# Projections as 32-column matmuls, and layer 1 with two exponentials a tile and two VectorE passes

## What is computed

```python
# layer 0: attention, softmax within blocks of 256 keys, 4 heads of 64
q, k, v = x @ Wq.T + bq, x @ Wk.T + bk, x @ Wv.T + bv
scores = clip(q k / sqrt(64), -10, 10);  scores = where(mask == 0, -10, scores)
ctx = softmax(scores over each 256 keys) @ v, summed over the 8 blocks
x1 = layernorm(x + layernorm(ctx @ Wo.T + bo + x) * gamma + beta)
# layer 1: graph attention
Wh = x1 @ W;  e = leaky_relu(s_i[:, None] + s_j[None, :], 0.2)
h = softmax(where(adj or diagonal, e, -inf)) @ Wh
out = layernorm(x1 + elu(h))
```

## Time and profile before

| | us |
|---|---|
| median of 3 runs | 4188.16 (4187.67 to 4192.0) |
| the profiled execution | 4188.57 |
| its span | 4186.4 |
| PE busy | 3834.5 (92%) |
| DVE busy | 3188.7 (76%) |
| ACT busy | 2463.5 (59%) |
| POOL busy | 2460.5 (59%) |
| mean granted TensorE clock | 0.970 of 2.4 GHz |

### The profile page before, as it was taken

How to read it: one execution, slowest core, us unless ns; L and a number is a source line. 1 busy time by engine, 2 the same in 40 slices (tenths; PEclk the granted TensorE clock), 3 DMA queues, 4 the chain that set the end, 5 groups by cost and what they waited for, 6 DMA issues and landing times. The chain is left out here.

```text
span 4186.4 us, 61904 instructions
## 1 busy us (share of the span) xinstructions
PE 3834.5 (92%) x20868; PEld 1843.7 (44%) x20868; DVE 3188.7 (76%) x3845; ACT 2463.5 (59%) x3554; POOL 2460.5 (59%) x1293
## 2 busy tenths in 40 slices
PE   6999999999999999999999999935888898888888
PEld 2333333333333333333333333225676676676766
DVE  6676776676677577677677667857998999989997
ACT  3565565556566566566566556624566566575666
POOL 2776776677677677677667667822434444344344
PEclk9999999999999999999999999967999999999999
DMA  5000000010001000000000000051011010110000
GB/s 205 1 31 11 21 31 11 11 42 11 11 12 41 11 12 31 21 11 31 11 21 32 11 11 21 11 208 39 26 45 52 21 46 25 41 51 21 31 31 31
DMA packets 106398, 140.44 MB, mean 34 GB/s; under 512 B 3793, under 2 KB 87633, under 8 KB 104017
## 3 DMA queue, kind: packets, MB, share of 16 engines
q1 hardware_dynamic: 104816, 135.80, 9.7%
q10 hardware_dynamic: 1248, 0.40, 0.1%
HBM read 102.63 MB, written 33.55 MB: 33 GB/s over the span
## 5 line engine op out<-in xcount | busy, mean ns | idle before, releaser
L368 ACT ACTIVATE probs<-probs 128x1024 f32<-128x1024 f32 x1024 | 1080.6, 1055 | 1006.0 <-DVE probs L614 975.4
L614 DVE SCALAR_TENSOR_TENSOR probs<-sc_ps,clip_hi 128x1024 f32<-128x1024 f32 x1024 | 1202.8, 1216 | 600.3 <-PE sc_ps L439 579.6
L267 POOL TENSOR_TENSOR psums<-probs 128x1024 f32<-128x1024 f32 x512 | 1244.6, 2452 | 164.1 <-ACT probs L368 164.1
L1102 PE MATMUL out_ps<-wh,e 128*128 128x257 f32 x4096 | 984.2, 394 | 208.4 <-ACT e L1029 201.5
L439 PE MATMUL sc_ps<-q_cols,k_cols 64*128 64x512 f32 x4096 | 1023.1, 618 | 24.4 <-DVE probs L614 12.4
L455 PE MATMUL ctx_ps<-probs,v_rows 128*32 128x512 f32 x8192 | 982.5, 597 | 1.2 <-DVE seg_ctx L537 1.2
L1102 PEld LDWEIGHTS out_ps<-wh,e 128*128 128x128 f32 x4096 | 789.7, 196 | 377.2 <-ACT e L1029 177.7
L278 POOL TENSOR_TENSOR ctx_t<-ctx_t,seg_ctx 128x1024 f32<-128x1024 f32 x224 | 532.1, 2376 | 671.4 <-DVE seg_ctx L537 671.3
L439 PEld LDWEIGHTS sc_ps<-q_cols,k_cols 64*128 64x128 f32 x4096 | 353.2, 186 | 697.1 <-issue 569.9
L903 POOL TENSOR_TENSOR e<-e,mask 128x512 f32<-128x512 f32 x160 | 247.6, 1547 | 549.2 <-DVE e L1224 549.2
L1029 ACT ACTIVATE e<-e 128x512 f32<-128x512 f32 x512 | 319.0, 623 | 404.9 <-DVE e L1240 292.8
(11 more groups left out here) (85 smaller groups left out, 2776.4 us busy)
## 6 DMA issues: line engine op xcount, KB each, us to landing
x_cols<-in_xT SPq DMA_DIRECT2D x8, 2048.0 KB, 10.1
probs<-in_adjT SPq DMA_DIRECT2D x16, 1024.0 KB, 8.3
x_rows<-in_x SPq DMA_DIRECT2D x32, 512.0 KB, 5.2
x<-res SPq DMA_DIRECT2D x32, 512.0 KB, 3.3
x_in<-x SPq DMA_DIRECT2D x8, 2048.0 KB, 11.0
x_res<-x SPq DMA_DIRECT2D x32, 512.0 KB, 4.4
out<-h SPq DMA_DIRECT2D x32, 512.0 KB, 3.2
e<-in_adjT SPq DMA_DIRECT2D x8, 1024.0 KB, 9.4
```

The costliest lines, as they stand in the source:

```text
L267: pool.tensor_tensor(psums[:, q % 2, pair, :], probs[:, (SJ * q) % RING, pair, :], probs[:, (SJ * q + 1) % RING, pair, :], ALU.add).then_i ...
L368: act.activation(probs[:, n % RING, pair, :], probs[:, n % RING, pair, :], ACT.Exp, scale=DH ** -0.5).then_inc(s_exp, 1)
L614: dve.scalar_tensor_tensor(out=probs[:, n % RING, pair, :], in0=sc_ps[:, p, :, :], scalar=-LIM, in1=clip_hi[:, j, c * CW:(c + 1) * CW][:, ...
L1102: last = pe.matmul(out_ps[:, bank(c, t), 0:F + 1], e[:, n % ERING, t * P:(t + 1) * P], wh[:, p, j, 1:F + 2], start=(j == 0), stop=(j == JB ...
```

## The change

**Layer 0, TensorE.** Every matmul of a projection with 128 columns of weights becomes four with 32, one for each quarter of the output partitions, with the same streamed operand. The result and what reads it stay as they were.

```diff
                     for k in range(KB):
-                        last = pe.matmul(prj_ps[:, :], wk[:, k, p * P:(p + 1) * P],
-                                         x_cols[:, k, c * CW:(c + 1) * CW], start=(k == 0), stop=(k == KB - 1))
+                        for g in range(P // QUAD):
+                            at = p * P + g * QUAD
+                            last = pe.matmul(prj_ps[quad(g), :], wk[:, k, at:at + QUAD],
+                                             x_cols[:, k, c * CW:(c + 1) * CW], start=(k == 0), stop=(k == KB - 1))
...
                     for z in range(HALVES):
-                        last = pe.matmul(prj_ps[:, 0:F], ctx_t[:, c % 2, z, t * P:(t + 1) * P], wo[:, z, :],
-                                         start=(z == 0), stop=(z == HALVES - 1))
+                        for g in range(P // QUAD):
+                            i = t * P + g * QUAD
+                            last = pe.matmul(prj_ps[quad(g), 0:F], ctx_t[:, c % 2, z, i:i + QUAD], wo[:, z, :],
+                                             start=(z == 0), stop=(z == HALVES - 1))
```

```diff
-                act.wait_ge(s_mm, count(b, STEPS, n + 1))
-                act.activation(e[:, n % ERING, :], low[:, p, c * CW:(c + 1) * CW], ACT.Identity,
-                               bias=s_fifth[:, p, j:j + 1]).then_inc(s_lin, 1)
+                act.wait_ge(s_max, count(b, STEPS, n + 1))
+                act.activation(e_low[:, n % LRING, :], low[:, p, c * CW:(c + 1) * CW], ACT.Exp,
+                               bias=s_fifth[:, p, j:j + 1]).then_inc(s_lo, 1)
+                act.wait_ge(s_mm, count(b, STEPS, n + 1))
+                act.activation(e[:, n % ERING, :], best[:, p, c * CW:(c + 1) * CW], ACT.Exp,
+                               bias=wh[:, p, j, 0:1]).then_inc(s_hi, 1)
...
-                        act.activation(e[:, n % ERING, :], e[:, n % ERING, :], ACT.Exp).then_inc(s_e, 1)
...
-                dve.wait_ge(s_lin, count(b, STEPS, n + 1))
-                dve.scalar_tensor_tensor(out=tile, in0=best[:, p, c * CW:(c + 1) * CW],
-                                         scalar=wh[:, p, j, 0:1], in1=tile, op0=ALU.add, op1=ALU.max)\
-                   .then_inc(s_max, 1)
+                dve.wait_ge(s_lo, count(b, STEPS, n + 1))
+                dve.wait_ge(s_hi, count(b, STEPS, n + 1))
+                dve.tensor_tensor(tile, tile, e_low[:, n % LRING, :], ALU.max).then_inc(s_max, 1)
...
-                        if j in ON_DVE:
-                            dve.wait_ge(s_max, count(b, STEPS, n + 1))
-                            dve.tensor_tensor(tile, tile, mask[:, j, c * CW:(c + 1) * CW], ALU.add)\
-                               .then_inc(s_log, 1)
+                        dve.wait_ge(s_max, count(b, STEPS, LRING + n + 1))
+                        dve.scalar_tensor_tensor(out=tile, in0=mask[:, j, c * CW:(c + 1) * CW], scalar=0.0,
+                                                 in1=tile, op0=ALU.max, op1=ALU.min).then_inc(s_e, 1)
```

```diff
+                dve.tensor_scalar(piece.bitcast(F32), piece, 0, 2 * BIG, ALU.is_gt, ALU.mult).then_inc(s_flag, 1)
+                dve.wait_ge(s_flag, i + 1)
                 dve.tensor_scalar(mask[:, 4 * q:4 * q + 4, c * CW:(c + 1) * CW],
-                                  stages[i % 4].rearrange("p (a i) -> p a i", a=4),
-                                  0, -BIG, ALU.is_le, ALU.mult).then_inc(s_mask, 1)
+                                  piece.bitcast(F32).rearrange("p (a i) -> p a i", a=4),
+                                  -BIG, None, ALU.add).then_inc(s_mask, 1)
...
+            def residual(b, c):
+                dve.wait_ge(s_elu, count(b, NC, c + 1))
+                dve.wait_ge(s_xr[c % 2], count(b, 16 * (NC // 2), 16 * (c // 2 + 1)))
+                dve.scalar_tensor_tensor(out=h[:, c % 2, :, :], in0=h[:, c % 2, :, :], scalar=-1.0,
+                                         in1=x_res[:, c % 2, :, :], op0=ALU.add, op1=ALU.add).then_inc(s_r, 1)
```

92 lines of the change are left out of this document (33 added, 59 removed).

## The result

The changed kernel takes **4034.72 us** in the median of 4 runs (4033.95 to 4037.52), beside 4189.58 (4187.67 to 4192.0) of the kernel before on the same chip: a ratio of 0.9631, interval 0.9615 to 0.9648, 155 us less. The forecast was 4018, with a range of 3985 to 4082.

What follows compares the result with a forecast made beforehand. TensorE was taken to bound layer 0, layer 1's D and the last batch, VectorE A to C. 4188.57 - 58 (layer 0) - 114 (VectorE) - 9 (TensorE) + 11 (mask) = 4018.6, given as 4018 us, range 3985 to 4082.

Steps and rivals of the forecast that it cites:

- Layer 0: Projections on TensorE: 32-column sets save the change of form, 0.195 us in 306 uses; -58 us, between 0 and -62.
- rival 4: Layer 0 projections: a set of four costs 0.43 us whatever it streams; 220 us longer, 4238, chance 0.05.
- Rival 3: Layer 0: 32-column sets lose against full instructions, 0.03 us in each of 1464 sets, 44 us: 4062; chance 0.04.
- Rival 2: Layer 0: time between forms belongs to any new group of 128-column weights and comes back elsewhere; no gain, 4076, chance 0.05.
- The mask: Before layer 1's first tile: one more VectorE pass for each of 16 pieces; +11 us, between 9 and 20.
- A: Layer 1, tiles 19 to 34, bound by VectorE: 19.8 + 4.7 + 9 x 2.26 = 44.8 instead of 51.1 us, plus 0.6 for ScalarE.
- D: Layer 1, tiles 3 to 18 with most preparations, bound by TensorE: stays at 34.9 us.
- B: Layer 1, tiles 35 to 50, bound by VectorE: 36.0 instead of 43.0 us, with 5 maxima, plus 0.6 for ScalarE.
- C: Layer 1, tiles 51 to 2, bound by VectorE: 34.7 instead of 39.5 us, 1 for the reduction included, plus 0.6 for ScalarE.
- last batch: Layer 1, nothing to prepare, bound by TensorE: from 30.3 to between 27.7 and 28.5 us a chunk; -9 us.
- Rival 1: Layer 1: VectorE waits for ScalarE, 3.6 instead of 0.6 us in 21 stretches; 63 us back, 4081, chance 0.12.
- Rival 5: Layer 1 without waits for ScalarE and the cap at 0.60 us: 14 and 13 us better, 3991; chance 0.12.

Runs made afterwards that it cites:

- 64-column kernel: The kernel before with each projection matmul cut into two of 64 columns; 4174.45 us, ratio 0.9963.
- mask_one_pass: The changed kernel with each mask piece made in one pass instead of two; 4025.33 us, ratio 0.9609.
- kernel with one moved maximum: The changed kernel with only the maximum of tile 18 moved in front of the reciprocals in the second chunk; 4027.37 us, ratio 0.9615.
- no_reduction: The changed kernel without GpSimd's reduction over partitions, each partition using its own maximum, for timing only; 4014.46 us, ratio 0.9577.

## Why the prediction was right or wrong

**Layer 0: right.** -58 forecast, -59.4 measured in the trace, -62 alone. k and q took 1.74 (forecast 1.75), v 1.75, o 0.89, the contexts behind 1.83. The price without a row, a set of 256 columns, was the lower of its bounds, and rival 4 (0.43 whatever streams) fell with it. Rival 3 fell too. The Trainium skill's 2.38 times for three column tiles (page "TensorE: Matmul & The Clock Gate", section "Measured speedup vs the span model") is not what this kernel shows: a set of four takes 0.43 us for 512 columns in f32, as one full instruction does, so the four lose nothing beside each other. Wrong in part was the cause. The prediction said that between two forms there is a time to pay, and that it was all of the 0.19. Of 0.197 us, 0.080 are the width of the first load, as the 64-column kernel shows. Rival 2's idea was thus right for a part of it, but not its consequence, as the narrow load stays narrow. The Trainium skill, page "TensorEngine Tiling (Array Packing)", section "Key Properties", says that changing the tiling mode drains TensorE. What is left, 0.093 us for leaving the full form and 0.097 for leaving the 64-column one, agrees with it; the page has no figure, and no run here tells a drain from another cause.

**The mask: right**, +11.2 for +11, and shown by `mask_one_pass`. Between the terms it was off by 1 us each way: the eight late pieces cost 10.1 (forecast 9) and the eight early ones 0.9 (forecast 1.6).

**A: the count was wrong.** The step "19.8 + 4.7 + 9 x 2.26" missed one: A has 10 `maximum` passes. The one of tile 18 stands behind the reciprocals in VectorE's order, on A's side of my cut. So D has one and not two. That is 2.26 more; tile passes at 1.20 a tile instead of 1.24 take 0.6 back, and the 0.6 us for ScalarE were not needed. Forecast 45.4 with that charge, measured 46.4: 7 us in 7 batches, and 1.6 more in the two A behind the loop's branch (47.8 and 49.3; before 53.1 and 51.8). The kernel with one moved maximum shows it: with 9, A takes 44.5.

**B: the reduction was put in the wrong stretch and at the wrong size.** The step "C: ... + 1 for the reduction that still runs beside it" should have been in B with 3.4 us, minus what TensorE allows. Forecast 36.6 with the charge, measured 39.6, 21 us in 7 batches, and this is the larger part of the miss. `no_reduction` gets 36.8, near the forecast, but by another bound: TensorE is busy 36.70 of it, at a granted clock of 0.95, where the prediction had it at "about 35 without waits, below VectorE". The row was there to be read: the L1224 of up to 3.8 us in the earlier trace rows was put down to masks, and in the trace of before it stands beside L896. The prediction said that GpSimd's tile work slows VectorE, and took the reduction for a small case of it. Instruction for instruction it is the largest one: there it holds a pass by 3.0 us, a residual alone by 2.1 and a mask by 0.9.

**C: right within 1.2 us**, 34.1 to 34.7 for 35.3, since the reduction isn't there. **D and the last batch: right**, 34.5 to 35.1 for 34.9, and 27.7 for 28.1. The errors of layer 1, +9 in A, +21 in B, -7 in C and -2 in the last batch, make 21 where the tiles missed by 20, and 1.4 us come back from layer 0. 4018 became 4034.7, and the range held it. The forecast of the time is thus good in part because layer 0 was, and because C erred the other way.

**Rival 1, ScalarE: no.** VectorE is idle for 0.06 us at most in the five A away from the loop's branch (1.3 and 2.9 in the two behind it), and in B and C for 1.0 to 1.9, all waits together, where the rival had 3.6 in each. D has more, 8.8 to 9.6 us, and the last batch 3.1 to 3.5 a chunk before its tail, where TensorE is the bound. In the first D 4.7 of them are waits for ScalarE, more than the 3 us a chunk that the prediction named as a sign of being wrong; they cost nothing there.

**Rival 5** had its conditions in part (cap at 0.60, no wait in A) and was overrun by the reduction.

## What to carry to other kernels

Matmuls that stand between groups of 32-column ones can be written in that form at no loss, and save the change of form on both sides; price it by the step from the start of one group to the start of the next. Where VectorE is the bound, work moved to GpSimd isn't free: count what it takes from VectorE, and look for each single long pass what stands beside it on GpSimd, and when that ends, before putting a share of them down to one cause. Before moving passes out of a stretch, list them in the engine's own order, since a cut at an event and a cut at a tile number differ by one.

## What the runs showed that was not expected

- The first step of a group behind another form is longer, and the excess goes with the width of its weight loads: 0.104, 0.051 and 0.024 us for 128, 64 and 32 columns. Leaving a form costs 0.094 and 0.097 us behind 128 and 64 columns.
- Four quarters' instructions written one quarter after the other still take 0.89 us for the 16, with starts 0.013 us apart; the contexts behind them take 0.020 us longer.
- A two-input addition of 128x512 on GpSimd (1.46 us) takes 0.96 us from the VectorE pass beside it (1.64 for 0.68). In the traces a pass held by one addition ends 0.55 us behind it in the median, whether the addition has 512 or 1024 columns (1.46 and 4.39 us). The reduction over partitions of 2048 columns (6.16 us) holds one pass, which in all seven batches of the change ends 1.98 us before the reduction's record does, and leaves the others alone.
- Before the reduction GpSimd shows 5.80 us in which it waits for nothing that the profile shows.
- Where the loop's branch is taken, TensorE's record of it lasts 6.4 to 6.9 us in the kernels read (0.08 where it isn't taken), and TensorE is idle for 2.7 to 3.2 us beside it. The D around it can be 2.9 us longer than another with the same work (37.5 and 34.6), or the A behind it, by 1.4 us at full clock and by 4.4 where TensorE's clock was 1.2 GHz for 6.8 us behind the branch.
